# A third buffer of turned rows in the linear attention, and the first dispatch's counting moved ahead of a barrier

## What is computed

```python
h = tok_ref(x, ...)                                  # 16 frames merged to 8
h = h + attn_ref(_layernorm(h), ...)                 # a state-space block
h = h + ffn_ref(_layernorm(h), w_fc, w_proj, w_gate) # 8 experts, the best 2 of each token
h = h + l1_attn_ref(_layernorm(h), W_qkv, b_qkv)     # linear attention with a decay mask
h = h + l1_ffn_ref(_layernorm(h), Wg, W1, b1, W2, b2)# 3 experts, 1 for each sequence

# inside ffn_ref
router_probs = softmax(x @ w_gate)
top_p, top_i = jax.lax.top_k(router_probs, 2)

# inside l1_attn_ref
q, k, v = jnp.split(x @ W_qkv + b_qkv, 3, axis=-1)
scores = jnp.einsum('bsd,btd->bst', q, k) / dim_sqrt * M
return jnp.einsum('bst,btd->bsd', scores, v)
```

## Time and profile before

| | us |
|---|---|
| median of 3 runs | 541.61 (540.09 to 542.0) |
| the profiled execution, its own time | 533.99 |
| its span, first to last instruction | 532.1 |
| PE busy | 485.7 (91%) |
| DVE busy | 356.3 (67%) |
| ACT busy | 271.4 (51%) |
| POOL busy | 228.8 (43%) |

### The profile page before, as it was taken

The page is one execution under the profiler, slowest core; times in us unless marked ns, Lnnn a source line. Parts: engine busy times, 40 slices in busy tenths (PEclk is TensorE's granted clock), DMA queues, the critical chain, the costliest instruction groups (busy, mean ns, idle before and its releaser), DMA issues.

```text
span 532.1 us, 15458 instructions
## 1 busy us (share of the span) xinstructions
PE 485.7 (91%) x5695; PEld 445.6 (84%) x5695; DVE 356.3 (67%) x967; ACT 271.4 (51%) x787; POOL 228.8 (43%) x332
## 2 busy tenths in 40 slices
PE   8999989999999229999999999999999997999993
PEld 7677767887887229999999999998887887999992
DVE  2666669998999585666556666563467765766771
ACT  2678878875677532333333333331457652554541
POOL 1245560003898614555555555533112215455531
PEclk9999999999999858999999999999999999999997
DMA  9994000006311101131221311210823323122210
GB/s 251 256 199 78 2 1 2 0 1 226 138 32 31 52 1 46 48 90 50 66 77 55 92 46 52 50 39 25 271 93 105 88 84 91 55 68 70 71 39 22
DMA packets 32381, 40.74 MB, mean 77 GB/s; under 512 B 7121, under 2 KB 27730, under 8 KB 32306
## 3 DMA queue, kind: packets, MB, share of 16 engines
q1 hardware_dynamic: 25586, 25.39, 17.6%
q0 software_dynamic: 5760, 12.98, 8.5%
q10 hardware_dynamic: 960, 1.38, 0.9%
HBM read 29.41 MB, written 10.32 MB: 75 GB/s over the span
## 4 chain that ended last, share of the span: by engine, by line
PE 57%; DVE 3%; issue 2%; ACT 2%; DMA 1%; POOLq 0%; POOL 0%; DVEq 0%; ACTq 0%
PE psum L1568 23%; PE psum L1580 20%; PE psum L1959 3%; PE psum L137 3%; PE psum L1963 2%; PE psum L1550 2%; PE psum L1970 1%; ACT rows_turned L1918 1%; PE psum L1716 1%; DVE hidden_room L1318 1%; PE psum L1951 1%; DMA rows_in<-y,token 1%; DVE token_in_tile_pairs L1323 0%; PE psum L1720 0%; PE psum L1725 0%
## 5 line engine op out<-in xcount | busy, mean ns | idle before, releaser
L1568 PE MATMUL psum<-rows_turned,expert_weights 64*128 64x128 f32 x2052 | 131.8, 275 | 0.0
L1580 PE MATMUL psum<-expert_second_weights,hidden_room 64*128 64x192 f32 x1368 | 125.4, 323 | 2.2 <-issue 2.2
L1568 PEld LDWEIGHTS psum<-rows_turned,expert_weights 64*128 64x128 f32 x2052 | 124.2, 188 | 0.3
L1580 PEld LDWEIGHTS psum<-expert_second_weights,hidden_room 64*128 64x128 f32 x1368 | 114.3, 187 | 2.7 <-issue 2.7
L1607 ACT ACTIVATE hidden_room<-psum 128x384 f32<-128x384 f32 x78 | 36.3, 491 | 83.6 <-PE psum L1568 80.3
L1532 POOL DMA_INDIRECT y<-rows_out,out_row_by_slot x39 | 45.5, 1166 | 74.3 <-DVE rows_out L1662 74.3
L1660 DVE COPY rows_out<-psum 128x192 f32<-128x192 f32 x39 | 14.0, 358 | 58.4 <-PE psum L1580 58.4
L1525 POOL DMA_INDIRECT rows_in<-x,token x39 | 42.9, 1099 | 22.4 <-issue 11.6
L855 PE MATMUL psum<-arena 97*128 97x512 f32 (+1 forms) x192 | 47.2, 400 | 0.8 <-ACT h L600 0.5
L855 PEld LDWEIGHTS psum<-arena 97*128 97x128 f32 (+1 forms) x192 | 35.7, 190 | 10.3 <-ACT h L600 0.9
L1593 ACT ACTIVATE rows_turned<-psum 128x192 f32<-128x192 f32 x57 | 19.0, 333 | 48.1 <-PE psum L1550 38.5
(11 more groups left out here) (284 smaller groups left out, 964.3 us busy)
## 6 DMA issues: line engine op xcount, KB each, us to landing
w_proj<-in_w_proj SPq DMA_DIRECT2D x8, 576.0 KB, 7.5
sz<-in_x SPq DMA_DIRECT2D x16, 192.0 KB, 7.8
w_fc<-in_w_fc SPq DMA_DIRECT2D x4, 768.0 KB, 18.0
w<-in_w SPq DMA_DIRECT2D x3, 576.0 KB, 4.3
w_fc<-in_w_fc SPq DMA_DIRECT2D x4, 384.0 KB, 16.8
x<-xf_tile SPq DMA_DIRECT2D x16, 96.0 KB, 1.6
expert_rows<-y SPq DMA_DIRECT2D x8, 192.0 KB, 3.8
hidden_room<-y SPq DMA_DIRECT2D x8, 192.0 KB, 4.6
```

What stands on the lines that cost most here:

```text
L1568: done = nc.tensor.matmul(ps_h[t.odd][half][:, ch, :], w_now[at, t.odd, first:first + P], xt[at, t.odd, block, :], start=block == 0 and ch ...
L1580: done = nc.tensor.matmul(ps_y[half], hid[at, t.odd, ch, :], w_down_now[at, t.odd, ch * D:(ch + 1) * D], start=ch == 0, stop=ch == HC - 1)
```

## The change

Three things.

1. The turned rows get a third buffer. Every use of `xt[..., t.odd, ...]` becomes `xt[..., t.i % 3, ...]`, and `take_turned` waits for the score of one tile earlier.
2. The head of the first dispatch becomes `count_pairs`, a stage at the end of the first block, ahead of the barrier: the floats of the picks, the marks, the scan, the own counts, the two products. So do GpSimd's two small memsets and ScalarE's two narrow copies, which go between the projection and the state-space stage in their engines' programs.
3. The tiles that cross the barrier move: `running` becomes a tile of its own that lives throughout, and the marks, picks, counts and `tiles` lie in `logits2`, which the linear attention fills later. An unused tile, `iota16`, goes. The count's semaphore `pairs_counted` outlives the barrier.

```diff
-                merge_frames(nc, dram, m, s, banks, projection, state_space(...))
+                mixing = state_space(nc, dram, m, s, w, ps, projection, -(-nc.sbuf_base // 32) * 32)
+                merge_frames(nc, dram, m, s, banks, projection, mixing, count_pairs(nc, m, s, banks, mixing))
...
                 projection.tensor(pe)
                 mixing.tensor(pe)
+                counting.tensor(pe)
...
                 projection.scalar(act)
+                counting.scalar(act)
                 mixing.scalar(act)
...
                 mixing.vector(dve)
+                counting.vector(dve)
...
+                counting.gpsimd(pool)
                 mixing.gpsimd(pool)
...
+def count_pairs(nc, m, s, banks, mixing):
...
+    def tensor(pe):
+        pe.wait_ge(turned, 2)
+        pe.wait_ge(own_set, 1)
+        nc.tensor.matmul(banks[1][:, 0:E1], m.ones16[:, :], own[:, :], start=True, stop=True).then_inc(m.pairs_counted, 1)
+        nc.tensor.matmul(banks[0][:, 0:E1], m.before16[:, :], own[:, :], start=True, stop=True).then_inc(m.pairs_counted, 1)
+
+    def scalar(act):
+        act.activation(m.ones16[:, :], c["ones"], ACT.Identity).then_inc(turned, 1)
+        act.activation(m.before16[:, :], c["before"], ACT.Identity).then_inc(turned, 1)
+
+    def gpsimd(pool):
+        nc.gpsimd.memset(m.running[:, 0, last:], 0.0).then_inc(zeroed, 1)
+        nc.gpsimd.memset(m.tiles[:, 0:1], 0.0).then_inc(zeroed, 1)
+
+    def vector(dve):
+        dve.wait_ge(mixing.logits_set, TILES)
+        nc.vector.tensor_copy(pick[:, :, :], m.pick[:, :, 0:2]).then_inc(pick_set, 1)
+        nc.vector.tensor_tensor(m.gate[:, :, 0], m.top[:, :, 1], m.top[:, :, 0], ALU.subtract)
+        dve.wait_ge(pick_set, 1)
+        nc.vector.tensor_tensor(m.one_hot[:, :, :], pick[:, :, :].rearrange("p i k -> p (i k)").unsqueeze(1).to_broadcast([P, E1, cols]),
+                                c["iota"][:, 0:E1].unsqueeze(2).to_broadcast([P, E1, cols]), ALU.is_equal).then_inc(one_hot_set, 1)
+        dve.wait_ge(one_hot_set, 1)
+        nc.vector.tensor_tensor_scan(m.running[:, 1:, :].rearrange(flat), m.one_hot[:, :, :].rearrange(flat), m.one_hot[:, :, :].rearrange(flat),
+                                     0.0, ALU.add, ALU.max).then_inc(running_set, 1)
+        dve.wait_ge(running_set, 1)
+        dve.wait_ge(zeroed, 2)
+        nc.vector.tensor_tensor(own[:, :], m.running[:, 1:, last], m.running[:, 0:E1, last], ALU.subtract).then_inc(own_set, 1)
...
-    xt = sb("rows_turned3", [HD + 1, 2, 2, P])
+    xt = sb("rows_turned3", [HD + 1, 3, 2, P])
...
-                need(act, s_mm, t.i - 1)
-                act.activation(xt[:, t.odd, :, :], ps_t, ACT.Identity).then_inc(t_out, 1)
+                need(act, s_mm, t.i - 2)
+                act.activation(xt[:, t.i % 3, :, :], ps_t, ACT.Identity).then_inc(t_out, 1)
```

More of the change, by code:

```diff
@@ L1211, in pair_dispatch @@
     last = cols - 1
-    one_hot = sb("one_hot", [P, E1, cols], BF16)
-    run = sb("running", [P, E1 + 1, cols])
-    own = sb("own_pairs", [P, E1], BF16)
+    one_hot, run, tiles = m.one_hot, m.running, m.tiles
     part = sb("tiles_part", [P, E1])
-    tiles = sb("tiles", [P, E1 + 1])
     ends = sb("tile_ends", [P, E1 + 1])
@@ L1241, in tensor @@
     def tensor(pe):
-        pe.wait_ge(turned, 2)
-        pe.wait_ge(one_hot_set, 1)
-        nc.tensor.matmul(ps_total, m.ones16[:, :], own[:, :], start=True, stop=True).then_inc(counted, 1)
-        nc.tensor.matmul(ps_before, m.before16[:, :], own[:, :], start=True, stop=True).then_inc(counted, 1)
         pe.wait_ge(token_in_tile_set, 1)
@@ L1258, in scalar @@
     def scalar(act):
-        act.activation(m.ones16[:, :], c["ones"], ACT.Identity).then_inc(turned, 1)
-        act.activation(m.before16[:, :], c["before"], ACT.Identity).then_inc(turned, 1)
         act.activation(minus_iota[:, :], c["iota"], ACT.Identity, scale=-1.0).then_inc(turned, 1)
@@ L1275, in gpsimd @@
     def gpsimd(pool):
-        nc.gpsimd.memset(run[:, 0, last:], 0.0).then_inc(zeroed, 1)
-        nc.gpsimd.memset(tiles[:, 0:1], 0.0).then_inc(zeroed, 1)
+        pass
     def vector(dve):
@@ L1958, in project @@
                 for ch, k in enumerate(chunk_rows):
-                    last = nc.tensor.matmul(ps_z[t.odd][:, part, :], m.w_qkv[0:k, ch, chunk_cols[part]], xt[0:k, t.odd, ch, :], start=ch == 0, stop=ch == 1)
+                    last = nc.tensor.matmul(ps_z[t.odd][:, part, :], m.w_qkv[0:k, ch, chunk_cols[part]], xt[0:k, t.i % 3, ch, :], start=ch == 0, stop=ch == 1)
             last.then_inc(z_mm, 1)
@@ L1962, in project @@
             for ch, k in enumerate(chunk_rows):
-                last = nc.tensor.matmul(ps_v[t.odd], xt[0:k, t.odd, ch, :], m.w_qkv[0:k, ch, 2 * D:], start=ch == 0, stop=ch == 1)
+                last = nc.tensor.matmul(ps_v[t.odd], xt[0:k, t.i % 3, ch, :], m.w_qkv[0:k, ch, 2 * D:], start=ch == 0, stop=ch == 1)
             last.then_inc(v_mm, 1)
@@ L1969, in score @@
             for ch, k in enumerate(chunk_rows):
-                last = nc.tensor.matmul(ps_s, xt[0:k, t.odd, ch, :], z[0:k, t.odd, ch, :], start=ch == 0, stop=ch == 1)
+                last = nc.tensor.matmul(ps_s, xt[0:k, t.i % 3, ch, :], z[0:k, t.odd, ch, :], start=ch == 0, stop=ch == 1)
             last.then_inc(s_mm, 1)
```

42 lines of the change are left out of this document (23 added, 19 removed).

## The result

| | before | changed |
|---|---|---|
| median of the runs, us | 540.09 (5 runs, 535.69 to 542.0) | 531.39 (5 runs, 531.14 to 534.61) |
| ratio, with its 95% interval | | 0.9899 [0.9854, 0.9944] |
| the profiled execution, its own time | 533.99 | 534.61 |
| its span | 532.1 | 532.7 |
| mean granted clock of that execution | 0.975 | 0.964 |

The change makes the kernel 1.0% faster, as was forecast in sign. The kernel before has two values here that it did not have when the prediction was made: 536.07 and 535.69, run beside the changed kernel. The first three runs alone, 541.61, 542.0 and 540.09, were the base of the forecast.

What follows compares the result with a forecast made beforehand. The chain that ends last is TensorE's expert work, 43% of the span and untouched, so gains come from outside it: counting -1.3 and third buffer -2.3 make -3.6, 541.6 to 538.0 us, range 535.6 to 540.3.

Steps and rivals of the forecast that it cites:

- The base: Whole kernel: median 541.6 us of the runs, 7.6 above the profiled 533.99, a difference carried over unchanged to the forecast.
- The third buffer: Linear attention: turned rows stop waiting for the score; gain 2.3 us, between 0.5 and 4.5.
- the tile with no moments asked for: Linear attention, first tile that waited, 0.9 us: nothing of VectorE's closes the loop there; gain 0.33 to 0.66, taken as 0.5.
- The loop over two steps: Linear attention: mask, moments, `var_eps`, turned rows, TensorE, next mask; 5.67 us per two steps, 0.16 saved per step.
- One longer and one shorter in turn: Sign of being right: attention steps of 2.84 us in the mean, perhaps alternating, since the loop spans two.
- TensorE's pace: Rival, attention: VectorE's and ScalarE's chain gives way, steps are 2.64 us; -5.8 in all, 535.8; chance 0.07.
- The counting: First dispatch moved ahead of the barrier: L1300 at 186.2 instead of 187.4; gain 1.25, taken as 1.3 us.
- B: Stage from the last best expert to L1336 (before: L1300), across the barrier: 6.02 us before, 4.47 changed.
- The sign of being wrong: At the barrier: over 2.1 us from TensorE's products to VectorE's first instruction would show the forecast wrong.
- The copies: ScalarE's two narrow copies ahead of the state-space stage: uncovered, they start it 0.4 us later, bounds 0 and 0.6.
- C: Stage from L1336 (before: L1300) to the first tokens, L1364, said to move unchanged with L1300; 10.13 us before, 10.27 changed.
- The late clock: Rival, first experts: TensorE's clock rises late, tiles run at the low level; 540.4 to 545.6 us; chance 0.07, 0.04 slower.

## Why the prediction was wrong in size and right in sign

**The base: this step failed.** The text said: "The runs have a median 7.6 us higher, which the profile does not explain; I carry the same difference over to it." The difference belonged to the three executions and not to the kernel. The same kernel had medians of 537.06, 536.15 and 535.92 in 34, 18 and 16 later runs. The profiled execution, 533.99, stood at a clock of 0.975, where eleven later runs have 534.75. The clocks of the first three runs are not listed, nor is their chip; 540 to 542 is what this kernel takes at 0.954 to 0.957, so that they ran at such a clock is likely and not shown. From 536.0 the same sum, 3.6, would have given 532.4, with 531.39 inside the forecast's own bounds. I had the clue: one execution 6.1 us, 1.1%, below the lowest of three that agree within 0.4% is no scatter. It should have been a case of its own: the base is the profile's level, the range then reaches down to about 529.

**The third buffer: right mechanism, 0.85 too small.** Forecast 2.3, measured 3.15.
- The wait that went was at the tile with no moments asked for: step 2 fell from 3.67 to 3.16, 0.51, forecast 0.5.
- The loop over two steps exists and is 5.61 long, forecast 5.67. In the rows above it is 3.11 from the mask (412.47) to L1995 (415.58) and 2.50 on to the next mask. Five pairs gave 0.39 each, 1.95, where the sum had 0.33.
- The last two steps are both 2.65, together 0.70 less: no moments hold up ScalarE at the end. The sum treated them like the others, 0.33. The step with the table load gave nothing (3.25 to 3.24). So twelve steps gained beside the first, where the sum had eleven.
- "One longer and one shorter in turn" was seen, 2.96 and 2.65. The short one is at TensorE's pace, for which the sum had 2.64. The variances behind the turned rows bring every step to it, so the rival of that name was wrong for this change and right about what lies behind the loop.

In the prediction the busy share gave TensorE 0.20 a step at the most, by the weight loads 0.51. What a step could give is 0.35: at 2.65 the busy share is 5.30 of 5.30 and the loads 4.98 of 5.30. The Trainium skill (Perfetto Trace Analysis, section Identifying the Most-Contended Engine) advises to go by the loads and not by the busy share. The trace agrees in that the busy share undersold the room, by 0.15; but the loads oversold it by as much, for at 2.65 they still show 0.16 a step that no edit here reached.

**The counting: right size, wrong reason.** B shrank by 1.55, forecast 1.65. Two errors offset each other. VectorE's part was shorter, 1.61 behind the last best expert instead of 2.0, since the CAST took 0.18 and not 0.51. And "the last store is issued ahead of the new end of the barrier's path" was false: it came at 188.28, 0.44 behind the products, because GpSimd's shift collided with the scan. What the barrier takes from its last comer on was forecast at 1.59; it took 1.62 from SyncE and, with the scan held back, 1.50 from TensorE. The sign of being wrong, over 2.1 from TensorE's products to VectorE, was just missed, at 2.06, and would have pointed at the late store.

**The copies: right.** 0.4 at their place. **C** was priced at nothing and is 0.14 to 0.22 longer; L1337 in it takes 0.33 (0.39 to 0.40 in the other kernels) beside GpSimd's memset, where its forerunner L1301 took 0.17. That is all of it. It does not reach the attention in this pair: from L1336 to the first L1995 it is 193.00, before 193.30.

**The sum of the stages** is -3.15 - 1.55 + 0.4 + 0.14 = -4.2, against the forecast's -3.6. The ratio's interval, 3.0 to 7.8 us of 537, holds both.

**The late clock: no case at the first experts, overlooked at the second.** The clock was back at 1.00 by 205 us and the first expert tile began at 207.95, so the first experts are as long as before. But the text let a shift ahead of the experts pass to the end unchanged, and looked for a fall at the first experts only. In the profile of the changed kernel the fall came at the second experts and took back 1.1 us. Whether the edit brings it on stays open.

## What to carry to other kernels

A profiled execution and a median are two draws, and a gap between them many times the usual spread says that something other than scatter may stand between; read the clock of each before choosing a base, and forecast the difference and the base apart. When a buffer is added, add up the loop that closes next, over as many steps as it spans, with the in-order queue of each engine in it, and then look at what moves to the head of that queue: here one reordering was worth 0.31 in every second step, but laid bare a table load. When work is moved up to a barrier, look at what it now runs beside, for the last comer can be an engine that the edit does not name. And read the clock of the stages behind an edit too: here a fall there took back a part of the gain in most profiles.

## What was not expected of the hardware

- **VectorE's scan holds up GpSimd.** A 128x1 TENSOR_SCALAR on GpSimd took 0.27 us alone and 0.72 to 0.73 when it started 0.03 behind a 0.69 scan with both inputs in SBUF; it ended 0.07 behind the scan. With the scan moved away it was 0.27. The Trainium skill (SBUF — State Buffer, section Who interferes with whom) says that a VectorE instruction with two SBUF inputs contends with a GpSimd instruction that reads SBUF, and that the ports which they share are an exclusive lock. For the scan the trace agrees in kind and size, and I should have weighed it: the edit puts the scan beside GpSimd's last work. It does not agree for every such pair: in the changed kernel the marks (L1242, two inputs in SBUF) ran for 0.43 from 186.14, beside GpSimd's TENSOR_TENSOR L1186 of 0.56 from 185.97, and neither is longer for it (0.42 and 0.56 with the other engine idle; spans on GpSimd are rough).
- **GpSimd's memsets and VectorE.** The CAST of 128x32 took 0.51 in the kernel before, where a memset ran beside it:

```profile
185.03 0.42 POOL L1698 MEMSET centring<- 97x384 f32 x1
```

  In its new place, with no memset beside it, it took 0.18. In the changed kernel it is L1337 that stands beside one, 0.33 long against 0.17 before:

```profile
190.42 0.42 POOL L1737 MEMSET centring<- 1x386 f32 x1
190.54 0.33 DVE L1337 TENSOR_SCALAR logits<-tiles_part_pairs 128x8 f32<-128x8 f32 x1
```

  The marks of the kernel before, a TENSOR_TENSOR, also stood beside a memset (L1288, 0.43) and were no longer than in their new place (0.43). No run took the memsets away, so this cause is not shown.
- **The clock falls while TensorE is busy.** Early in the program, with all of 24 to 28 us busy, the clock fell to 0.50 and stayed there up to some 120 us in one execution. In seven other profiles it fell for 3 to 10 us, at two places that recur, from 30 and from 79 to 81 us; in four, that of the kernel before among them, it did not fall at all ahead of 170 us. The Trainium skill (TensorE: Matmul & The Clock Gate, section What's actually happening) has a low state that is the default and that activity releases. That the moment varies from run to run agrees; that it fell under a busy share of 1.00 in the records (loads 2.39 of 4.00) is not what one would read out of it. What makes it fall was not tried.
